# A fused recurrent block on one core: the next tile's normalised, turned tokens come by channel from memory

## The reference

```python
x = L0_attn_x                                   # (2, 1024, 256)
xn = _layernorm(x, axis=-1)                     # (x - mean) / sqrt(var + 1e-5), no gain
s = _L0_attn_ref(xn, ...)                       # token shift, 5 mixes, recurrence, group norm, W_o
g = _silu(_L0_ffn_ref(xn, ...))                 # 2:4 sparsified hidden units
x = x + s * g
xn = _layernorm(x, axis=-1)
s = _L1_attn_ref(xn, ...)                       # gated state-space layer
g = _silu(_L1_ffn_ref(xn, ...))
x = x + s * g
```

## Time and profile before

| what | value |
|---|---|
| median of 3 runs | 766.62 us (766.07 to 769.03) |
| profiled execution, its own time | 767.01 us |
| span of the profiled execution | 765.3 us, so 1.7 us lie around it |
| busy in the span: PE, DVE, ACT, POOL | 735.6, 506.1, 325.8, 76.1 us |
| mean granted clock of PE | 0.99 |
| moved by DMA | 39.77 MB |

### The profile page before, as it was taken

How to read it: one execution, slowest core, us unless ns; L and a number is a source line. 1 busy time by engine, 2 the same in 40 slices (tenths; PEclk the granted TensorE clock), 3 DMA queues, 4 the chain that set the end, 5 groups by cost and what they waited for, 6 DMA issues and landing times.

```text
span 765.3 us, 18468 instructions
## 1 busy us (share of the span) xinstructions
PE 735.6 (96%) x7316; PEld 602.7 (79%) x7316; DVE 506.1 (66%) x1177; ACT 325.8 (43%) x659; POOL 76.1 (10%) x85
## 2 busy tenths in 40 slices
PE   4888999999999999999999999999999999999997
PEld 3666678877888788887888878888778878888686
DVE  3877679737797367945678467874679737795143
ACT  1312565126642366214752057512664236631570
POOL 6201011001011011000110001100011101100020
PEclk9879999999999999999999999999999999999999
DMA  8800320015000150002400032000500015000220
GB/s 291 318 1 15 116 39 3 1 30 153 2 3 1 44 139 2 3 2 71 112 2 2 3 121 60 3 1 30 147 8 3 0 44 140 2 3 1 96 57 15
DMA packets 33938, 39.77 MB, mean 52 GB/s; under 512 B 20352, under 2 KB 27968, under 8 KB 32192
## 3 DMA queue, kind: packets, MB, share of 16 engines
q1 hardware_dynamic: 33856, 38.49, 16.8%
HBM read 32.12 MB, written 6.36 MB: 50 GB/s over the span
## 4 chain that ended last, share of the span: by engine, by line
PE 93%; DVE 4%; issue 1%; ACT 1%; DMA 0%; POOL 0%; DVEq 0%; SPq 0%; ACTq 0%; POOLq 0%
PE psum L1275 72%; PE psum L1364 4%; PE psum L1474 2%; PE psum L1459 2%; PE psum L1324 1%; PE psum L1335 1%; PE psum L1485 1%; PE psum L1683 1%; PE psum L1512 1%; PE psum L1610 1%; PE psum L1384 1%; PE psum L1556 1%; PE psum L1420 1%; PE psum L1403 1%; PE psum L1427 1%
## 5 line engine op out<-in xcount | busy, mean ns | idle before, releaser
L520 ACT ACTIVATE BC<-psum 64x256 f32<-64x256 f32 x128 | 81.2, 634 | 3.5 <-PE psum L1275 1.8
L1275 PE MATMUL psum<-xnT,sb_f_gate 128*128 128x256 f32 x256 | 66.6, 404 | 1.8 <-issue 1.0
L1275 PE MATMUL psum<-xnT,sb_f_up 128*128 128x256 f32 x256 | 62.3, 385 | 0.0
L1275 PE MATMUL psum<-xn1T,sb_n_gate 128*128 128x256 f32 x256 | 61.4, 383 | 0.0
L1275 PE MATMUL psum<-xn1T,sb_n_up 128*128 128x256 f32 x256 | 60.5, 379 | 0.0
L1275 PEld LDWEIGHTS psum<-xnT,sb_f_gate 128*128 128x128 f32 x256 | 48.7, 198 | 11.6 <-issue 2.9
L1275 PEld LDWEIGHTS psum<-xn1T,sb_n_up 128*128 128x128 f32 x256 | 48.6, 190 | 6.6
L1275 PEld LDWEIGHTS psum<-xn1T,sb_n_gate 128*128 128x128 f32 x256 | 47.3, 190 | 6.5
L1275 PEld LDWEIGHTS psum<-xnT,sb_f_up 128*128 128x128 f32 x256 | 47.1, 189 | 6.6 <-issue 0.2
L868 DVE TENSOR_TENSOR kT<-kT,dec 128x256 f32<-128x256 f32 x56 | 25.2, 450 | 39.3 <-PE psum L1364 31.8
L1275 PE MATMUL psum<-sb_n_down,hidB 128*128 128x256 f32 x224 | 49.5, 379 | 0.0
(11 more groups left out here) (203 smaller groups left out, 1496.4 us busy)
## 6 DMA issues: line engine op xcount, KB each, us to landing
cs_row<-cs_dram SPq DMA_DIRECT2D x8, 1024.0 KB, 5.2
x_dram<-gate SPq DMA_DIRECT2D x8, 512.0 KB, 2.8
cs_half<-cs_dram SPq DMA_DIRECT2D x16, 256.0 KB, 6.3
hidB<-x_dram SPq DMA_DIRECT2D x8, 512.0 KB, 7.9
X<-in_x SPq DMA_DIRECT2D x9, 256.0 KB, 2.8
x<-in_x SPq DMA_DIRECT2D x8, 256.0 KB, 2.7
out_tokens<-thFB SPq DMA_DIRECT2D x8, 256.0 KB, 2.2
sb_w_rkvgo<-in_w_rkvgo SPq DMA_DIRECT2D x1, 1280.0 KB, 5.7
```

Of the source, the lines that this page charges most:

```text
L520: ins = a_.activation(cols[:, par, 2 * pair:2 * pair + 2, :], src[64 * par:64 * par + 64, :, s, :], ACT.Identity)
L1275: ins = t_.matmul(ps(t, name)[first_row:first_row + rows, col:col + n], w, x, start=(k == 0), stop=(k == len(ws) - 1))
```

## The change

`xnT` of tiles 1 to 8 (tile 8 is a repetition of tile 7 that nothing uses) is no longer made by transposing. The input also comes as `x_turned`, laid out by channel outside the timed program. SP loads it as `XT [128, 2, 256]` with the same wait as `X`. `next_stats` now writes mean and variance to `token_stats`, POOL overwrites the variance there with `rstd`, and SP stores the 2 KB of pairs to `row_dram` and loads them back to all partitions as `rows [128, 256 tokens, 2]` (256 KB). `next_normed` then subtracts and multiplies on DVE in the turned layout, and `next_turned` and `next_copied` are gone. Tile 0 is still transposed.

```diff
-FILLS = [["xT", "mix_w", "dw", "w0", "k", "mix_g0", "L0", "k0T", "p3g", "F0"],
+FILLS = [["mix_w", "dw", "w0", "k", "mix_g0", "L0", "k0T", "p3g", "F0"],
...
+            def channels(tile):
+                return A["x_turned"][bass.ds(tile * P, P), :].rearrange("p (h t) -> p h t", h=CH)
+
+            def token_rows(a):
+                wait(rstd_ready, a.count(3, 2))
+                wait(rows_loaded, a.count(16, 16))
+                sp_.dma_start(A["row_dram"].rearrange("(q p two) -> p q two", q=NQ, p=P),
+                              token_stats[:, :, :]).then_inc(rows_stored, 16)
+                wait(rows_stored, a.count(16, 16))
+                sp_.dma_start(rows[:, :, :].rearrange("p t two -> p (t two)"),
+                              A["row_dram"].partition_broadcast(P)).then_inc(rows_loaded, 16)
...
                     wait(xn_ready, a.count(1, 1))
                     sp_.dma_start(X[:, :, :], tokens("x", a.at() * T if last else a.next().at() * T)).then_inc(x_loaded, 16)
+                    sp_.dma_start(XT[:, :, :], channels(a.at() if last else a.next().at())).then_inc(xT_loaded, 16)
...
                     sp_.dma_start(Xrow.rearrange("p q c d -> p (q c) d"),
                                   x_dram.rearrange("(c p d) -> p c d", p=P, d=SD)).then_inc(X_rows, 16)
+                    if a:
+                        token_rows(a)
                     wait(out_ready, b.count(1, 2))
...
-                    rsqrt(a.count(3, 2))
+                    rsqrt(a.count(3, 2), token_stats[:, :, 1])
...
-                def next_copied():
-                    act.wait_ge(carry_ready, a.count(1, 1))
-                    xnT_copy(a.next())
...
                 def next_stats():
                     dve.wait_ge(x_loaded, a.count(16, 32))
-                    norm_stats(X)
+                    norm_stats(X, token_stats)
 
                 def next_normed():
-                    norm_apply(X, xn, a.count(3, 2), xn_ready)
-
-                    d.tensor_scalar(xnT[:, :, 0:1], xnT[:, :, T:T + 1], keep[:, bass.ds(a.next().at(), 1)], None,
-                                    ALU.mult).then_inc(carry_ready, 1)
+                    dve.wait_ge(rows_loaded, a.count(16, 32))
+                    dve.wait_ge(xT_loaded, a.count(16, 16))
+                    did(d.tensor_tensor(XT[:, :, :], XT[:, :, :], rows[:, :, 0].unsqueeze(1).to_broadcast([P, CH, T]),
+                                        ALU.subtract))
+                    did(d.tensor_scalar(xnT[:, :, 0:1], xnT[:, :, T:T + 1], keep[:, bass.ds(a.next().at(), 1)], None,
+                                        ALU.mult))
+                    after()
+                    d.tensor_tensor(xnT[:, :, 1:T + 1], XT[:, :, :], rows[:, :, 1].unsqueeze(1).to_broadcast([P, CH, T]),
+                                    ALU.mult).then_inc(xn_ready, 1)
...
                 def gates_0():
-                    wait_freed(pe, a, "xT")
+                    pe.wait_ge(xn_ready, a.count(1, 1))
                     ffn_p(a, 0)
...
-                def next_turned():
-                    pe.wait_ge(xn_ready, a.count(1, 2))
-                    transposes(a.next(), "xT", xn)
```

More of the change, by code:

```diff
@@ L82 @@
 EXTRA = [len(names) - (PER[b] if b < RING else 0) for b, names in enumerate(FIRST_FILLS)]
-FILLED_BEFORE = [EXTRA[b] + (NT * PER[b] + (b == BANK["xT"]) if b < RING else (NT - 1) * PER[b]) for b in range(BANKS)]
+FILLED_BEFORE = [EXTRA[b] + (NT if b < RING else NT - 1) * PER[b] for b in range(BANKS)]
 class Tile:
@@ L122, in build_block @@
         W = {n: sb("sb_" + n, list(A[n].shape)) for n in A
-             if n not in ("x", "out", "cs_dram", "x_dram", "w_mix2b", "w_dec2")}
+             if n not in ("x", "out", "x_turned", "row_dram", "cs_dram", "x_dram", "w_mix2b", "w_dec2")}
         W["w_mix2b"], W["w_dec2"] = sb("sb_mix2b", [NQ * DMIX, C]), sb("sb_dec2", [NQ * DDEC, C])
@@ L140, in build_block @@
         xn = sb("xn", [P, NQ, C])
+        XT = sb("XT", [P, CH, T])
+        token_stats = sb("token_stats", [P, NQ, 2])
+        rows = sb("rows", [P, T, 2])
         xnT = sb("xnT", [P, CH, T + 1])
@@ L228, in build_block @@
         x_loaded = sem("x_loaded")
+        xT_loaded = sem("xT_loaded")
+        rows_stored = sem("rows_stored")
+        rows_loaded = sem("rows_loaded")
         const_ready = sem("const_ready")
@@ L393, in one @@
                         out_stored, 16)
-            for s in (X_rows, X_stored, cs_stored, cs_loaded, out_stored):
+            for s in (X_rows, X_stored, cs_stored, cs_loaded, out_stored, rows_loaded):
                 sp_.sem_inc(s, 16)
@@ L411, in _ @@
             load(["n_gate", "n_up", "n_down"], "ffn1")
+            token_rows(Tile(None, 0, first=True))
             with sp_.Fori(1, NT - 1) as it:
@@ L431, in _, with rsqrt @@
             g.memset(rstd[:, :], 1.0).then_inc(const_ready, 1)
-            def rsqrt(count, out=rstd, var=var_eps, n=NQ):
+            def rsqrt(count, out=rstd[:, :], var=var_eps, n=NQ):
                 pool.wait_ge(var_ready, count)
-                g.tensor_tensor(out[:, :], var[:, :], half_neg[:, 0:n], ALU.pow).then_inc(rstd_ready, 1)
+                g.tensor_tensor(out, var[:, :], half_neg[:, 0:n], ALU.pow).then_inc(rstd_ready, 1)
             pool.wait_ge(const_ready, 2)
@@ L779, in norm_apply @@
                 for q in range(NQ):
-                    ins = d.tensor_scalar(dst[:, q, :], src[:, q, :], meanvar[:, 2 * q:2 * q + 1], rstd[:, q:q + 1],
+                    ins = d.tensor_scalar(dst[:, q, :], src[:, q, :], meanvar[:, q, 0:1], rstd[:, q:q + 1],
                                           ALU.subtract, ALU.mult)
@@ L787, in _ @@
             dve.wait_ge(x_loaded, 16)
-            norm_stats(X)
+            norm_stats(X, meanvar)
             norm_apply(X, xn, 1, xn_ready)
@@ L947, in differences @@
             def differences(t):
-                wait_freed(dve, t, "xT")
+                if t.first:
+                    wait_freed(dve, t, "xT")
+                else:
+                    dve.wait_ge(xn_ready, t.count(1, 1))
                 did(d.tensor_tensor(dxT[:, :, :], xnT[:, :, 0:T], xnT[:, :, 1:T + 1], ALU.subtract))
@@ L1853, in _layout @@
                       "time_decay", "time_faaaa", "ln_gamma", "ln_beta")])
-    out = {"x": v[pre + "x"].reshape(TOKENS, C),
+    x = v[pre + "x"].reshape(TOKENS, C)
+    out = {"x": x,
+           "x_turned": x.reshape(NT, T, CH, P).transpose(0, 3, 2, 1).reshape(NT * P, CH * T),
            "vecs": vecs.reshape(len(VEC), CH, P).transpose(2, 0, 1).reshape(P, len(VEC) * CH),
```

20 lines of the change are left out of this document (7 added, 13 removed).

## The result

| kernel | median us (lowest to highest, runs) | ratio to before | profiled execution, span |
|---|---|---|---|
| before | 766.49 (765.42 to 770.09, 6) | | 767.01, 765.3 |
| changed | 763.52 (762.00 to 763.87, 6) | 0.9952 [0.993, 0.9974] | 762.50, 760.8 |

The account below looks back on a forecast made before the run. The prediction took PE's instructions to bound the rounds: seven times 0.44 us saved is 3.1 us, everything else costed at nothing, so 767.0 - 3.1 = 763.9 us profiled and 763.5 us for the median, range 762.4 to 766.7.

Parts of the forecast that it names:

- The bound and the distance: PE's instructions end rounds 1 to 7; four transpositions before `out_1` cost 0.44 us by distance, 3.1 us over seven rounds.
- rival A: On PE, each removed transposition gains its full 0.273 us duration, 28 times, 7.6 us: 759.0 us; chance 0.06.
- Round 0 gives nothing: In round 0 `out_0` waits for DVE's `mixed_w`, so removing PE's transpositions gains nothing; bounds nothing and 0.44 us.
- DVE's added work: Before the gates DVE does 1.61 us instead of 0.96, hidden by its idle time and `mixed_w`'s lead; cost zero.
- lower bound: Each of the two new 128x512 DVE operations takes 0.69 us, the value the prediction took.
- upper bound: Each new DVE operation takes 1.39 us: still free in rounds 1 to 7, `out_0` 1.1 us late once.
- The range's ceiling: Upper end of the predicted time for the whole kernel, 766.7 us, from the upper ends of B and C.
- SP's transfers: Three more a round; rows land by 291.8, DVE asks near 325: 33 us slack; store 1.6 us, load 6.3.
- How far it scatters: Rounds differ by 0.5 us, one cause POOL's `cs_row` mask lengthening first-level `kT` from 0.46 to 0.90: 762.4 to 764.6.
- B: Rival: rounds give the gain back, through late masks or another engine ending them; about 766.6 us; chance 0.09.
- C: Rival: PE's clock falls once more in round 0, costing 1.8 to 3.2 us: 765.3 to 766.7; chance 0.09.
- D: Rival: added transfers delay `cs_half`, so the mask covers first-level `kT` each round; 776.5 us at 2.0 us delay; chance 0.06.

## Why the prediction was right, step by step

**The bound and the distance.** The forecast of 763.5 us met 763.52, on the ground given: PE ends the rounds, and a transposition in a stream costs the distance to its successor. Doubling gave 0.44 us a round, removing gave it back (with 0.1 us from another place, see below), and rival A, the full duration, would have shown 7.6 us either way. The trace shows 273 ns as the duration of one, and a row of four at 0.44 us is 0.11 us each as a price.

**A term that was missed, and the scatter.** The stretch from `kT` shrank by 0.52 us, not 0.44, because an issue gap of PE 26 us before the transpositions shrank when they went; the prediction has no term for it. Seven times 0.52 is 3.6 us. Five comparisons of kernels without the transpositions against before gave 2.3 to 3.3 us by the medians (2.97, 2.32, 3.17, 3.33, 2.34). In the stretch ahead of `kT`, six rounds each of eleven executions without them average 37.37 us and of three with them 37.31; if this 0.06 is real (its uncertainty is 0.04), it gives 0.4 us back. The rest is within the intervals, which reach 0.9 to 1.7 us to either side. So the exact hit is partly luck: a sum of 3.1 was made of 3.6 and something given back.

**Why the profiled executions differ by 4.5.** From before's first `kT` of round 1 to its last `out_1` it is 4.44 us more than after: 7 times 0.52 are 3.64; rounds 1 and 6 of before were longer by 0.43 and 0.28 from the mask, rounds 1 and 7 of the changed kernel by 0.10 and 0.30, net 0.31; the changed kernel's six stretches ahead of `kT` were 37.21 to 37.26 us, 0.45 in all under before's, which no other execution repeated (the changed kernel again: 37.22 to 37.65); its cause is open. Together 4.40.

**Round 0 gives nothing.** Right: 99.40 against 99.43 us at the first `kT`. Behind DVE's added work 0.33 us of idle time was left ahead of `mixed_w`, where the prediction had 0.25.

**DVE's added work.** Right at the lower bound, 0.68 and 0.69 us. At the upper bound, two operations more, rounds 1 to 7 would have been as free as predicted, but round 0 would have cost 2.35 us instead of 1.1, since the clock falls there (to 0.50 for 3.4 us in the kernel with two more). The range's ceiling covered that.

**SP's transfers.** The step was right and one term mis-sized: the store of the rows lands after 3.0 us in the median and 7.4 at most, not 1.6, the price of `cs_dram`; their load lands after 4.2 us, not 6.3. With 33 us of slack it costs nothing, and with 19 us less still nothing.

**How far it scatters.** Here the reasoning failed in part. `kT`'s length does not reach the round in full: at 0.60 us it costs nothing, at 0.73 0.10 to 0.13, at 0.90 0.28 and at 1.31 0.67, so the first 0.17 us are covered. Taking the collisions away did not lower the median clear of its scatter, and most of the scatter of a round lies ahead of `kT`, of unknown cause.

**Rivals.** B: excluded as a loss, since `out_1` moved with PE's products. C: not met by the change; its mechanism was met by two more operations. Before, the granted clock was at 0.50 twice in round 0, from 33.4 to 40.2 and from 50.4 to 57.3 us; in the changed kernel it was from 33.2 to 40.0 and from 50.3 to 57.1, and then not again until the last round. D: the transfers did not move the mask late, because `XT` is issued early; made true, it cost 2.3 us over before and 5.6 over its sibling with a late mask, but it would have been mistaken in its place (second level) and its price a round.

## What to carry to other kernels

Price a removed instruction by the distance that it adds between its neighbours on the engine that ends the stage, and look for covers on all other engines; here that gave the time to a microsecond. Split a round at an event inside it and compare the halves over all rounds: one half was constant to 0.04 us in a kernel's undisturbed rounds, which showed a gap of 0.1 us that no median could. Where an engine already waits in the first, unfilled round, more work ahead of that wait can cost the clock as well as the wait; here it did in both kernels that had it, with the clock at 0.50 for 3.4 us behind waits of 2.00 and 4.18 us.

## What the runs showed of the hardware

**POOL's mask holds up more of DVE's operations than `kT`, but not all.** In the profile of the changed kernel's second measurement (start, us):

```profile
188.41 2.01 POOL L494 TENSOR_SCALAR_AFFINE_SELECT cs_row<-cs_row 128x2048 f32<-128x2048 f32 x1 [34.87 <-DMA cs_half<-cs_dram]
188.50 1.95 DVE L790 TENSOR_SCALAR var_eps<-token_stats 128x2 f32<-128x2 f32 x1
```

An addition to two numbers per partition takes 0.17 us in other rounds and 1.95 here, until the mask is over. It has only one input in SBUF. In all profiles together it began under the mask 18 times and was held to the mask's end each time. Why it is held is not shown by any trace. It cost little: DVE idles some 2 us ahead of `kT` (1.86 and 1.90 in the earlier trace rows), and that round's period was 90.81 us. Other operations pass. With the mask late (first chip), the two for `gate`, with one operand in PSUM, run beside it in 1.28 us, as they do elsewhere:

```profile
208.91 1.28 DVE L1098 SCALAR_TENSOR_TENSOR gate<-gate,psum 128x512 f32<-128x512 f32 x2
```

```profile
209.33 2.01 POOL L499 TENSOR_SCALAR_AFFINE_SELECT cs_row<-cs_row 128x2048 f32<-128x2048 f32 x1 [17.49 <-DVE rT L887]
```

The second of the two began under the mask and took 0.68 us, and so it was in all 19 cases on record.

**Executions come in two levels of PE's clock.** Of before's runs on the third chip twelve have a mean granted clock of 0.990 or 0.991 and a median of 767.28 us, four of 0.996 to 0.998 and 765.77. On the second chip ten of 16 were at the higher level (0.995 or more), on the first five of 23 (0.997 or more), which can be a part of why before's plain median differs by 1.3 us between these two chips. It is not the whole: the first chip's medians by level are 767.0 and 766.0 us, the second's 766.8 and 765.0. With ten or more fillers all 17 executions had 0.996 or more. Two profiles show where the levels come from: the changed kernel's, at 0.991, has two low stretches in round 0, at 0.50 from 33 to 40 and from 50 to 57 us, and that with the transpositions put back, at 0.998, has only one, at 0.50 from 56 to 59 us, without any filler.
